# Attention over 32 sequences: the five order tables of the engines are rewritten

## The chip, the cores and the metric

The kernel runs on one core of a Trainium2 chip. The metric is the device time of one execution in microseconds, from the first to the last instruction with what lies around them; lower is better.

## What is computed

A one-layer language model tower on 32 sequences of 512 tokens, 256 channels wide. The reference, cut to what matters here:

```
h = emb_weight[x] + 2 * (lora_A[:, x].T @ lora_B.T)            # token embedding with a LoRA part
n = layernorm(h)
q, k, v = split(n @ Wqkv + bqkv)                                # 16 heads of 16 channels
local  = softmax(q k' / 4 within 64 positions) @ v
global = softmax(q k'[first 64 keys] / 4) @ v[first 64]
g = sigmoid(n @ Wg + bg)
h = h + ((1 - g) * local + g * global) @ Wout + bout
x2 = layernorm(h)
k_idx, k_probs = top_k(softmax(x2 @ router_w.T), 2)             # 8 experts, capacity limited
h = h + x2 + sum over the 2 experts of k_probs * (silu(x2 @ w1) @ w2)
```

## The kernel before, in words

The program has three stages. A short one prepares weights and tables. Then the attention stage works through the 32 sequences. Then the expert stage runs the feed-forward part over the slots of the 8 experts. Only the attention stage is touched.

In the attention stage one sequence is cut into small steps: TensorE computes tiles of scores twice, once to find the row maxima (step `max`, lines 699 to 721, 20 a sequence) and once transposed for the exponential (step `exp`, lines 741 and 748, 20 a sequence). VectorE reduces the first kind (L993, L997), ScalarE takes the exponential of the second (L903, L907), GpSimd cuts the local band out of it with two affine selects (step `sel`, L568 and L570, 16 a sequence), and TensorE multiplies with the values (step `out`, L769, L774). Around that stand the projections (`values` L795 and L800, `qk` L858, `project` L831), the transposes (`xn_t` L852 and others), the layer norms on VectorE, and the routing of the sequence two steps back.

GpSimd also issues the indirect DMAs. For each sequence there are eight gathers (step `gather`: an even argument fetches 128 rows of the LoRA table into `la`, L582, an odd one 128 rows of the embedding into `emb_t`, L585) and eight scatters (step `scatter`, L592: 128 entries of 8 bytes into the slot table). That is 16 indirect DMAs a sequence. Its other steps are `hold` (L620, an addition), `qk3` (L608), `mix` (L601), and `rstd1` and `rstd2` (L611 and L614, a power).

The order of the work is written out by hand. Each of the five engines has a table, and one pass over it issues the steps of up to seven sequences: `cur` is sequence i, `nxt` i + 1, `far` i + 2, `next` i + 3, `prev` i - 1, `past` i - 2 and `old` i - 3. The program unrolls the tables:

```
for i in range(-3, SEQ + 4):
    for flag, stage, arg in ORDER[name]:
        if 0 <= i + REL[flag] < SEQ:
            yield stage, arg, i + REL[flag]
```

So each engine's instructions stand in a fixed order, and an engine that meets a semaphore it has to wait for holds up all that is behind it on that engine. The semaphores themselves come from the data: s_ready (TensorE to VectorE, a `max` tile is complete), max_done (back), st_ready and exp_done (the same pair with ScalarE), sel_done, pv_ready and so on. In steady state one pass of a table is one sequence; below it is called a pass.

Of the kernel before, what the change touches and what calls it, by code (L numbers as in the profile page):

```python
# [89 lines left out]
def build(nc, x, emb, lora_a, lora_b, wqkv, bqkv, wout, bout, wg, bg, rw, w1, w2, y):  # L90
# [20 lines left out]
    with outer:  # L111
# [247 lines left out]
        with ExitStack() as mem:  # L359
# [8 lines left out]
            hb = tmp("hb", [P, QB, D])  # L368
# [107 lines left out]
                ("cur", "exp", 16), ("prev", "x2_t", 0), ("nxt", "max", 7), ("prev", "x2_t", 1), ("cur", "exp", 17),
                ("nxt", "m_rows", 0), ("nxt", "max", 8), ("prev", "router", None), ("cur", "out", 9), ("cur", "exp", 18),
                ("nxt", "max", 9), ("nxt", "values", 0), ("nxt", "max", 10), ("prev", "logits", None), ("cur", "exp", 19),
                ("nxt", "values", 1), ("cur", "out", 10), ("cur", "out", 11), ("nxt", "m_rows", 1), ("nxt", "values", 2),
                ("nxt", "max", 11), ("far", "xn_t", 0), ("far", "xn_t", 1), ("nxt", "exp", 0), ("nxt", "max", 12), ("far", "qk", 0),  # L480
                ("nxt", "exp", 1), ("far", "qk", 1), ("far", "qk", 2), ("nxt", "max", 13), ("far", "qk", 3), ("nxt", "exp", 2),
                ("nxt", "max", 14), ("cur", "mix", 0), ("nxt", "exp", 3), ("nxt", "out", 0), ("nxt", "max", 15), ("cur", "mix", 1),
                ("nxt", "exp", 4), ("nxt", "max", 16), ("cur", "mix", 2), ("nxt", "exp", 5), ("nxt", "max", 17), ("nxt", "out", 1),
                ("nxt", "m_rows", 2), ("nxt", "exp", 6), ("nxt", "max", 18), ("cur", "mix", 3), ("nxt", "exp", 7),
# [17 lines left out]
            ORDER["dve"] = (
                ("nxt", "max", 5), ("nxt", "cut", (0, 1)), ("prev", "scale2", 1), ("prev", "scale2", 2), ("prev", "scale2", 3),
                ("nxt", "cut", (0, 2)), ("nxt", "max", 6), ("far", "lora", 1), ("nxt", "cut", (0, 3)), ("nxt", "max", 7),
                ("far", "stats1", 0), ("nxt", "max", 8), ("far", "stats1", 1), ("prev", "shift", None), ("far", "var1", None),
                ("nxt", "max", 9), ("nxt", "kg", 1), ("nxt", "cut", (1, 0)), ("cur", "gates", None), ("nxt", "cut", (1, 1)),
                ("nxt", "gate1", None), ("nxt", "cut", (1, 2)), ("past", "rank", 5), ("far", "scale1", 0), ("prev", "logits", None),
                ("nxt", "cut", (1, 3)), ("nxt", "max", 10), ("far", "scale1", 1), ("far", "scale1", 2), ("far", "scale1", 3),
                ("nxt", "kg", 2), ("prev", "top", 0), ("nxt", "max", 11), ("nxt", "max", 12), ("far", "qk", 0), ("far", "zgate", 0),
                ("far", "qk", 1), ("prev", "top", 1), ("far", "qk", 2), ("nxt", "max", 13), ("far", "qk", 3), ("nxt", "max", 14),  # L510
                ("cur", "mix", (0, 0)), ("nxt", "cut", (2, 0)), ("cur", "mix", (0, 1)), ("nxt", "cut", (2, 1)), ("nxt", "max", 15),
                ("prev", "top", 2), ("cur", "mix", (1, 0)), ("cur", "mix", (1, 1)), ("nxt", "max", 16), ("nxt", "cut", (2, 2)),
                ("nxt", "cut", (2, 3)), ("prev", "top", 3), ("cur", "mix", (2, 0)), ("cur", "mix", (2, 1)), ("nxt", "max", 17),
                ("nxt", "max", 18), ("cur", "mix", (3, 0)), ("cur", "mix", (3, 1)), ("nxt", "max", 19), ("prev", "top", 4),
                ("nxt", "cut", (3, 0)), ("nxt", "cut", (3, 1)), ("nxt", "cut", (3, 2)), ("prev", "rank", 0), ("nxt", "cut", (3, 3)),
                ("nxt", "kg", 3), ("far", "max", 0), ("prev", "rank", 1), ("nxt", "gate2", None), ("far", "kg", 0),
                ("far", "max", 1), ("prev", "rank", 2), ("far", "zgate", 1), ("cur", "project", 0), ("far", "max", 2),
                ("next", "la_cut", 0), ("prev", "rank", 3), ("cur", "project", 1), ("next", "la_cut", 1), ("prev", "top", 5),
                ("cur", "stats2", 0), ("far", "max", 3), ("cur", "stats2", 1), ("prev", "rank", 4), ("cur", "var2", None),
# [1156 lines left out]
```

How the kernel before makes its waits and increments, by code:

```python
    def sync(self):  # L77
        self.eng.wait_ge(self.sem, self.n * self.turn + self.k)
# [5 lines left out]
def need(eng, sem, count):  # L84
    if not (isinstance(count, int) and count <= 0):
        eng.wait_ge(sem, count)
# [100 lines left out]
                @block.sync  # L188
# [5 lines left out]
                    full = VG - 1
                    whole = lora_a[:, 0:full * GT].rearrange("r (g c) -> g r c", g=full)
                    for c in range(0, GT, PIECE):
                        if c + PIECE > VOCAB - full * GT:
                            need(sp, dve_base, 1)
                        sp.dma_start(la_src[0:R * full, c:c + PIECE],
                                     whole[:, :, c:c + PIECE]).then_inc(lora_in, 16)
                    sp.dma_start(la_src[R * full:R * VG, 0:VOCAB - full * GT], lora_a[:, full * GT:VOCAB]).then_inc(lora_in, 16)
                    for c, (first, end) in enumerate(PARTS):
                        sp.wait_ge(step_copied, part_chunks[c])
                        sp.dma_start(lora_grid[:, 0:VG // 2, first:end, :], la_dst[:, 0:VG // 2, first:end, :]).then_inc(scratch_out, 16)
                    sp.wait_ge(dve_made, 3)
                    sp.dma_start(table.rearrange("(p j) w -> p j w", p=P), tab[:, :, :]).then_inc(scratch_out, 16)
                    sp.dma_start(x2_rows[N:N + P, :], zpad[:, :]).then_inc(scratch_out, 16)
                    sp.dma_start(y[N:N + P, :], zpad[:, :]).then_inc(scratch_out, 16)
                    sp.wait_ge(scratch_out, 16 * (3 + 2 * len(PARTS)))
```

## Time and profile before

| | |
|---|---|
| runs | 3893.07, 3895.12, 3898.6 us; median 3895.12 us |
| the profiled execution | 3882.32 us, span 3880.6 us |
| attention stage | about 112 us to about 2290 us of the span |
| copies of a sequence's ids on GpSimd (L577), one a pass | at 364.22 us and, 25 passes later, at 2057.27 us |
| one pass in steady state | (2057.27 - 364.22) / 25 = 67.7 us |
| mean granted TensorE clock | 0.952 |

The page divides the span in 40 slices of 97 us; the first 23 are the preparation and the attention stage, the rest is the expert stage. In the rows below a time in brackets behind a row is how long the engine sat idle before it, and what ended that wait. A row of windows gives for one stretch the busy time of each engine, then the granted TensorE clock (1.00 is 2.4 GHz, 0.50 is 1.2 GHz), the share of the DMA engines and GB/s.

### The profile page before, as it was taken

Reading aid. Unit: us, or ns where it says so; the run is one execution under the profiler, and the core shown is the slowest. Engines: PE = TensorE matmul, PEld = TensorE weight load, DVE = VectorE, ACT = ScalarE, POOL = GpSimd, SP = SyncE. Lnnn points to the kernel's source line nnn. Section 1 sums busy time; section 2 is a strip of 40 time slices with the busy share of each in tenths; the row PEclk is TensorE's granted clock in tenths of the full one; section 3 lists DMA queues with packets and bytes.
Section 4 is the critical chain, followed back from the end, with each engine's and each line's share of the span. In section 5 each row is a group of like instructions: output and inputs, shape, how many; then the busy total and the mean of one; then the engine's idle time right before and its main releaser. Section 6 shows DMA issues by size and latency. Waiting matters only on the chain. (4 is left out here: it accounts for less than half of the span.)

```text
span 3880.6 us, 117579 instructions
## 1 busy us (share of the span) xinstructions
PE 3481.5 (90%) x47537; PEld 2753.0 (71%) x47537; DVE 2172.5 (56%) x5392; ACT 1868.3 (48%) x3086; POOL 2324.1 (60%) x2599
## 2 busy tenths in 40 slices
PE   2898889888888888888899849999999999999998
PEld 1555555555555555555555539999999999999998
DVE  3576767767676776767677634343434344443333
ACT  0455555555555555555555624343444444444343
POOL 5566777777777777777776645444544444444443
PEclk7899999999999999999999969999999999999999
DMA  4354544445454444545454323232323233222222
GB/s 142 123 157 117 163 122 151 130 138 139 128 152 123 150 133 135 144 125 149 124 154 130 109 87 65 50 68 46 71 48 72 48 69 72 46 51 45 45 45 41
DMA packets 242540, 398.31 MB, mean 103 GB/s; under 512 B 34572, under 2 KB 150748, under 8 KB 242044
## 3 DMA queue, kind: packets, MB, share of 16 engines
q1 hardware_dynamic: 168540, 297.43, 25.0%
q0 software_dynamic: 70512, 91.16, 13.8%
q8 instruction: 345, 5.65, 0.6%
q10 hardware_dynamic: 3008, 2.95, 0.2%
q14 instruction: 135, 1.11, 0.1%
HBM read 198.55 MB, written 192.88 MB: 101 GB/s over the span
## 5 line engine op out<-in xcount | busy, mean ns | idle before, releaser
L1388 POOL DMA_INDIRECT out_y<-out_t,tok_out x264 | 425.7, 1612 | 747.3 <-DMA out_y<-out_t,tok_out 405.0
L1534 ACT ACTIVATE act<-psS 128x512 f32<-128x512 f32 x528 | 316.9, 600 | 882.1 <-PE psS L1462 880.9
L1596 DVE TENSOR_TENSOR h_lo<-act,h_hi 128x512 fp32r<-128x512 f32 x528 | 367.2, 695 | 562.3 <-ACT h_hi L1535 543.8
L993 DVE TENSOR_REDUCE negm<-psS 128x4 f32<-128x640 f32 x512 | 418.8, 818 | 452.3 <-remote 276.3
L903 ACT ACTIVATE pl<-psS 128x896 f32<-128x896 f32 x512 | 467.7, 913 | 379.9 <-PE psS L741 372.0
L568 POOL TENSOR_SCALAR_AFFINE_SELECT pl<-pl 128x512 f32<-128x512 f32 x512 | 354.3, 692 | 448.4 <-ACT pl L903 446.2
L1497 PE MATMUL psO<-w_hi,h_hi 128*128 128x256 f32 x2112 | 598.8, 284 | 0.8 <-DVE h_lo L1596 0.8
L1497 PE MATMUL psO<-w_lo,h_hi 128*128 128x256 f32 x2112 | 588.7, 279 | 0.0
L1497 PE MATMUL psO<-w_hi,h_lo 128*128 128x256 f32 x2112 | 587.6, 278 | 0.0
L1462 PE MATMUL psS<-xg_hi,w_hi 128*128 128x256 f32 x1984 | 551.7, 278 | 0.0
L1462 PE MATMUL psS<-xg_hi,w_lo 128*128 128x256 f32 x1984 | 551.5, 278 | 0.0
L1462 PE MATMUL psS<-xg_lo,w_hi 128*128 128x256 f32 x1984 | 551.3, 278 | 0.0
L1497 PEld LDWEIGHTS psO<-w_hi,h_hi 128*128 128x128 f32 x2112 | 397.0, 188 | 1.1 <-DVE h_lo L1596 1.0
L1497 PEld LDWEIGHTS psO<-w_lo,h_hi 128*128 128x128 f32 x2112 | 397.0, 188 | 0.0
L1497 PEld LDWEIGHTS psO<-w_hi,h_lo 128*128 128x128 f32 x2112 | 395.5, 187 | 0.0
L1462 PEld LDWEIGHTS psS<-xg_hi,w_hi 128*128 128x128 f32 x1984 | 375.1, 189 | 0.0
L1462 PEld LDWEIGHTS psS<-xg_lo,w_hi 128*128 128x128 f32 x1984 | 372.5, 188 | 0.0
L1462 PEld LDWEIGHTS psS<-xg_hi,w_lo 128*128 128x128 f32 x1984 | 372.4, 188 | 0.0
L699 PE MATMUL psS<-K,Q 96*32 96x160 bf16 (+2 forms) x8192 | 260.8, 237 | 105.7 <-DVE negm L993 71.2
L1628 DVE TENSOR_SCALAR out_t<-psO,wt_all 128x256 f32<-128x256 f32 x264 | 127.8, 484 | 360.7 <-PE psO L1497 355.8
L699 PEld LDWEIGHTS psS<-K,Q 96*32 96x32 bf16 x8192 | 165.6, 98 | 231.2 <-DVE negm L993 109.0
L570 POOL TENSOR_SCALAR_AFFINE_SELECT pl<-pl 128x512 f32<-128x512 f32 x512 | 328.0, 641 | 0.0
(232 smaller groups left out, 7728.6 us busy)
## 6 DMA issues: line engine op xcount, KB each, us to landing
qk_scr<-qk SPq DMA_DIRECT2D x64, 768.0 KB
Q<-qk_scr SPq DMA_DIRECT2D x128, 384.0 KB
K<-qk_scr SPq DMA_DIRECT2D x128, 384.0 KB
qk_scr<-qk SPq DMA_DIRECT2D x64, 512.0 KB
qk_scr<-qk SPq DMA_DIRECT2D x64, 256.0 KB
h_rows<-held SPq DMA_DIRECT2D x32, 512.0 KB
hb<-h_rows SPq DMA_DIRECT2D x32, 512.0 KB
x_rows<-x SPq DMA_DIRECT2D x32, 512.0 KB
```

The source lines that it names most:

```text
L568: pool.affine_select(out=cols[:, :, 0:P], in_=cols[:, :, 0:P], compare_op=ALU.is_ge, fill=0.0, base=0, pattern=[[0, 4], [1, P]], channel_m ...
L570: pool.affine_select(out=cols[:, :, P:WIN], in_=cols[:, :, P:WIN], compare_op=ALU.is_ge, fill=0.0, base=0, pattern=[[0, 4], [-1, P]], chan ...
L699: pe.matmul(psS[SUB * c:SUB * (c + 1), 2 + a, q % 2 * BAND + lo:q % 2 * BAND + hi], Q[0:ROWS, 4 * g + 2 * v + a, (4 * q + c) * SUB:(4 * q ...
L903: act.activation(pl[:, v, half, :, lo:hi], psS[:, 0:2, lo:hi], ACT.Exp, scale=SCALE).then_inc(exp_done, 1)
L993: dve.tensor_reduce(negm[:, g, 0, v, :, 2 * half:2 * half + 2], psS[:, 2:4, 0:2 * BAND].rearrange("p a (q u) -> p a q u", u=BAND), AX.X, A ...
L1388: pool.indirect_dma_start(out=y[:, :], in_=out_t[:, tile.out, s, :], in_offset=None, out_offset=bass.IndirectOffsetOnAxis(ap=tok_out[:, ti ...
L1462: last = pe.matmul(psS[:, f // 2, (f % 2) * 256:(f % 2) * 256 + cols], w[:, tile.par, k, fs], x[:, k, 0:cols], start=(k == 0 and n == 0), ...
L1497: last = pe.matmul(psO[:, s, 0:D], h_[:, f, ts], w[:, tile.par, f, :], start=(f == 0 and n == 0), stop=(f == FT - 1 and n == 2))
L1534: act.activation(act32[:, b, :, 0:cols], src, ACT.Silu)
L1596: dve.tensor_tensor(h_lo[:, 2 * b:2 * b + 2, 0:cols], act32[:, b, :, 0:cols], h_hi[:, 2 * b:2 * b + 2, 0:cols].bitcast(F32), ALU.subtract) ...
L1628: dve.tensor_scalar(out_t[:, tile.out, s, :], psO[:, s, 0:D], wt_all[:, bass.ds(tile.h0 + s, 1)], None, ALU.mult).then_inc(out_done, 1)
```

## The change

All five tables are replaced by new ones. They name the same steps for each sequence: no instruction of a sequence is added or taken away, no tile or semaphore changes, and the unrolling loop is the same. What changes is the order of the steps on each engine, and with it which sequences meet in a pass. In the new table of GpSimd no `gather` or `scatter` stands directly behind another. The core of the diff, of the table of GpSimd:

```diff
             ORDER["pool"] = (
...
-                ("cur", "sel", 17), ("next", "gather", 0), ("far", "rstd1", None), ("cur", "sel", 18), ("next", "gather", 1),
-                ("past", "scatter", 2), ("next", "gather", 2), ("next", "gather", 3), ("past", "scatter", 3), ("next", "gather", 4),
...
+                ("old", "scatter", 7), ("cur", "sel", 15), ("cur", "sel", 16), ("next", "gather", 0), ("cur", "sel", 17),
+                ("cur", "sel", 18), ("next", "gather", 1), ("far", "rstd1", None), ("next", "gather", 2), ("far", "hold", 0),
+                ("next", "gather", 3),
             )
```

What this makes of the program, from the steady part of the attention stage (new line numbers are 3 higher). First GpSimd, from the ids' copy that opens a sequence's gathers; L568 and L570 are the selects of one `sel`. Before:

```order
L577 COPY id_cur<-ids 128x4
L582 DMA la<-lora_rows,id_cur 128x16
L611 TENSOR_TENSOR rstd<-var,neg_half 128x4
L568 AFFINE_SELECT pl<-pl 128x4x128
L570 AFFINE_SELECT pl<-pl 128x4x128
L585 DMA emb_t<-in_L_tok_emb_weight,id_cur 128x256
L592 DMA slot_table<-entry,slot_i 41984x2
L582 DMA la<-lora_rows,id_cur 128x16
L585 DMA emb_t<-in_L_tok_emb_weight,id_cur 128x256
L592 DMA slot_table<-entry,slot_i 41984x2
L582 DMA la<-lora_rows,id_cur 128x16
L620 TENSOR_TENSOR held<-h,bout_b 128x256
```

And now, from the second gather on:

```order
L588 DMA emb_t<-in_L_tok_emb_weight,id_cur 128x256
L614 TENSOR_TENSOR rstd<-var,neg_half 128x4
L585 DMA la<-lora_rows,id_cur 128x16
L623 TENSOR_TENSOR held<-h,bout_b 128x256
L588 DMA emb_t<-in_L_tok_emb_weight,id_cur 128x256
L623 TENSOR_TENSOR held<-h,bout_b 128x256
L595 DMA slot_table<-entry,slot_i 41984x2
L571 AFFINE_SELECT pl<-pl 128x4x128
L573 AFFINE_SELECT pl<-pl 128x4x128
L595 DMA slot_table<-entry,slot_i 41984x2
```

Before, six indirect DMAs stand in a row, then one addition and a seventh. Now the same stretch has a power, an addition or two selects between any two of them.

The second place is GpSimd in the middle of a pass. Before, a gather and a scatter stood side by side there:

```order
L585 DMA emb_t<-in_L_tok_emb_weight,id_cur 128x256
L592 DMA slot_table<-entry,slot_i 41984x2
L620 TENSOR_TENSOR held<-h,bout_b 128x256
L568 AFFINE_SELECT pl<-pl 128x4x128
L570 AFFINE_SELECT pl<-pl 128x4x128
L592 DMA slot_table<-entry,slot_i 41984x2
```

And now:

```order
L588 DMA emb_t<-in_L_tok_emb_weight,id_cur 128x256
L571 AFFINE_SELECT pl<-pl 128x4x128
L573 AFFINE_SELECT pl<-pl 128x4x128
L595 DMA slot_table<-entry,slot_i 41984x2
L571 AFFINE_SELECT pl<-pl 128x4x128
L573 AFFINE_SELECT pl<-pl 128x4x128
```

The two are two selects apart. There were two more such pairs in a pass, both of two scatters; they are apart too. In the first passes, where most steps of the table fall away because their sequence does not exist, a few gathers still follow each other, and behind the last sequence 17 scatters stand in a row (16 before).

The third place is TensorE where the next sequence is normalised and projected. L800 is the last of `values`, L699 begins a `max` tile, L741 an `exp` tile; the transposes of the normalised rows (L852) and the projections (L858) follow a few rows on. Before:

```order
L774 MATMUL psO<-pg,V 32x512 x4
L807 MATMUL psX<-identb,m_cut 24x128 x4
L800 MATMUL psX<-wv_sb,xn_t 64x128 x4
L699 MATMUL psS<-K,Q 32x160 x10
L699 MATMUL psS<-K,Q 32x128
```

And now:

```order
L777 MATMUL psO<-pg,V 32x512 x4
L803 MATMUL psX<-wv_sb,xn_t 64x128 x4
L744 MATMUL psS<-Q,K 32x96
L744 MATMUL psS<-Q,K 32x128
L744 MATMUL psS<-Q,K 32x160 x2
```

The first `exp` tile of the next sequence now stands ahead of the `max` tile and the transposes; the transposes and the projections behind them keep their place among their neighbours.

## Rows read from the trace of the kernel before

**Rows 1.** The page: busy time by engine, and the granted clock in 40 slices.

```profile
PE 3481.5 (90%) x47537; PEld 2753.0 (71%) x47537; DVE 2172.5 (56%) x5392; ACT 1868.3 (48%) x3086; POOL 2324.1 (60%) x2599
...
PEclk7899999999999999999999969999999999999999
```

**Rows 2.** Windows: 25 passes of the attention stage; 200 us of the expert stage.

```profile
364.22:2057.27 1693.05, 1501.61 (x26752) 935.27 (x26752) 1179.15 (x3177) 930.52 (x1451) 1223.04 (x1576) 0.95 0.48 138
```

```profile
2400.00:2600.00 200.00, 197.22 (x1689) 196.82 (x1688) 81.11 (x160) 84.83 (x156) 92.21 (x71) 0.99 0.31 59
```

**Rows 3.** The page's groups: GpSimd's DMAs and a matmul of the expert stage.

```profile
L1388 POOL DMA_INDIRECT out_y<-out_t,tok_out x264 | 425.7, 1612 | 747.3 <-DMA out_y<-out_t,tok_out 405.0
...
L1462 PE MATMUL psS<-xg_hi,w_hi 128*128 128x256 f32 x1984 | 551.7, 278 | 0.0
```

**Rows 4.** Timeline of GpSimd in one pass: start, length, instruction, idle before.

```profile
1019.47 0.98 POOL L585 DMA_INDIRECT emb_t<-in_L_tok_emb_weight,id_cur  x1 [0.17 <-issue]
1020.76 1.01 POOL L592 DMA_INDIRECT slot_table<-entry,slot_i  x1 [0.31 <-issue]
...
1046.30 1.03 POOL L585 DMA_INDIRECT emb_t<-in_L_tok_emb_weight,id_cur  x1 [0.18 <-issue]
1047.63 1.15 POOL L592 DMA_INDIRECT slot_table<-entry,slot_i  x1 [0.30 <-issue]
...
1052.95 0.98 POOL L582 DMA_INDIRECT la<-lora_rows,id_cur  x1 [0.30 <-issue]
1053.95 0.74 POOL L620 TENSOR_TENSOR held<-h,bout_b 128x256 f32<-128x256 f32 x1
```

**Rows 5.** Timeline of TensorE in the same pass.

```profile
1019.88 0.28 PE L715 MATMUL psS<-mask,identb 128*32 128x128 bf16 x7
...
1023.15 0.46 PE L699 MATMUL psS<-K,Q 96*32 96x96 bf16 x16 [1.06 <-DVE negm L993]
...
1051.97 0.26 PE L715 MATMUL psS<-mask,identb 128*32 128x128 bf16 x3 [0.46 <-issue]
```

**Rows 6.** Timeline of VectorE in the same pass.

```profile
1022.27 0.82 DVE L993 TENSOR_REDUCE negm<-psS 128x4 f32<-128x640 f32 x1 [2.34 <-remote]
...
1055.07 0.82 DVE L993 TENSOR_REDUCE negm<-psS 128x4 f32<-128x640 f32 x1 [6.13 <-remote]
```

**Rows 7.** Windows over 27 trains of six DMAs: one of them, and the sum.

```profile
1046.35:1054.60 8.25, 6.22 (x75) 3.43 (x73) 2.59 (x12) 2.76 (x6) 6.71 (x7) 1.00 0.54 131
...
sum 219.87, PE 157.06 PEld 89.35 DVE 59.92 ACT 57.59 POOL 178.29; mean PE 5.82 PEld 3.31 DVE 2.22 ACT 2.13 POOL 6.60
```

**Rows 8.** The same over 27 pairs of DMAs: the sum.

```profile
sum 78.60, PE 64.87 PEld 45.18 DVE 41.27 ACT 6.81 POOL 64.33; mean PE 2.40 PEld 1.67 DVE 1.53 ACT 0.25 POOL 2.38
```

**Rows 9.** The same over 27 DMAs that stand alone: the sum.

```profile
sum 43.20, PE 38.52 PEld 24.83 DVE 29.10 ACT 21.07 POOL 38.33; mean PE 1.43 PEld 0.92 DVE 1.08 ACT 0.78 POOL 1.42
```

**Rows 10.** The same over 25 DMAs behind one addition: one, and the sum.

```profile
376.67:378.27 1.60, 1.25 (x13) 0.48 (x14) 0.00 (x0) 0.00 (x0) 0.93 (x1) 0.50 0.00 1
sum 40.00, PE 28.60 PEld 14.93 DVE 0.92 ACT 7.10 POOL 23.20; mean PE 1.14 PEld 0.60 DVE 0.04 ACT 0.28 POOL 0.93
```

**Rows 11.** Waits over the 25 passes: us in total, times, longest.

```profile
PE psS L699 <- DVE negm L993: 56.8, 69, 1.1
PE psX L817 <- DVE mix L1096: 13.0, 25, 0.5
```

```profile
DVE negm L993 <- remote: 242.4, 49, 8.0
```

**Rows 12.** Timeline of TensorE where the queries and keys are projected.

```profile
1124.21 3.60 PE L858 MATMUL psX<-xn_t,wqk 128*128 128x512 f32 x4
1127.74 0.46 PE L741 MATMUL psS<-Q,K 102*32 102x96 bf16 x16
1128.13 3.70 PE L858 MATMUL psX<-xn_t,wqk 128*128 128x512 f32 x8
```

**Rows 13.** Windows: a stretch at the lower clock.

```profile
1056.00:1059.40 3.40, 3.40 (x30) 1.79 (x30) 0.83 (x1) 1.51 (x3) 2.21 (x3) 0.53 0.14 41
```

**Rows 14.** GpSimd's selects over the 25 passes: busy, mean ns, idle before.

```profile
L568 POOL TENSOR_SCALAR_AFFINE_SELECT pl<-pl 128x512 f32<-128x512 f32 x400 | 277.3, 693 | 337.7 <-ACT pl L903 335.6 <-issue 1.5
```

More of the change, by code:

```diff
@@ L476, in build @@
[L476 to L484, printed above, removed]
@@ new lines, in build @@
+                ("nxt", "exp", 0), ("nxt", "max", 11), ("far", "xn_t", 0), ("far", "xn_t", 1), ("nxt", "exp", 1),
+                ("nxt", "max", 12), ("far", "qk", 0), ("far", "qk", 1), ("nxt", "max", 13), ("far", "qk", 2), ("far", "qk", 3),
+                ("nxt", "exp", 2), ("nxt", "max", 14), ("cur", "mix", 0), ("nxt", "out", 0), ("nxt", "max", 15), ("nxt", "exp", 3),
+                ("cur", "mix", 1), ("nxt", "exp", 4), ("nxt", "max", 16), ("cur", "mix", 2), ("nxt", "exp", 5), ("nxt", "out", 1),
@@ L487, in build @@
+                ("nxt", "max", 17), ("nxt", "m_rows", 2), ("nxt", "exp", 6), ("cur", "mix", 3), ("nxt", "exp", 7),
+                ("nxt", "max", 18), ("nxt", "out", 2), ("nxt", "exp", 8), ("nxt", "max", 19), ("cur", "attn_t", 0),
+                ("cur", "attn_t", 1), ("nxt", "exp", 9), ("prev", "ahead", None), ("far", "max", 0), ("nxt", "out", 3),
+                ("nxt", "m_rows", 3), ("far", "max", 1),
             )
             ORDER["act"] = (
-                ("cur", "exp", 11), ("cur", "evac", (1, 0)), ("cur", "exp", 12), ("far", "embed", None), ("cur", "exp", 13),
@@ L504, in build @@
[L504 to L519, printed above, removed]
-                ("prev", "top", 6), ("far", "max", 4), ("next", "lora", 0), ("far", "cut", (0, 0)), ("cur", "scale2", 0),
+                ("prev", "mix", (2, 0)), ("prev", "mix", (2, 1)), ("past", "top", 4), ("cur", "max", 17), ("cur", "gates", None),
@@ L539, in build @@
+                ("cur", "qk_write", (0, 2)), ("cur", "qk_write", (1, 0)), ("cur", "qk_write", (1, 1)), ("cur", "qk_write", (1, 2)),
+                ("cur", "load", 0), ("prev", "m_out", 2), ("prev", "m_in", 2), ("old", "y", None), ("prev", "m_out", 3),
+                ("cur", "load", 1), ("prev", "m_in", 3), ("cur", "hold", None), ("cur", "load", 2), ("cur", "m_out", 0),
+                ("cur", "m_in", 0), ("cur", "load", 3), ("past", "x2", None), ("cur", "m_out", 1),
             )
```

76 lines of the change are left out of this document (46 added, 30 removed).

## The prediction

> **What bounds the kernel now.** I began with the page. TensorE is busy 90% of the span and no other engine above 60% [rows 1], so the question is where TensorE loses the rest. The windows answer it by stage: in the expert stage it is busy 197.22 of 200 us at full clock, in 25 passes of the attention stage 1501.61 of 1693.05 us at a mean clock of 0.95 [rows 2]. So a pass of 67.7 us holds 191.44 / 25 = 7.66 us of idle TensorE, and a clock of 0.95 between the levels 1.00 and 0.50 is 10% of the pass, 6.8 us, at the lower one. The expert stage has GpSimd's indirect DMAs too, of 1.6 us each, and TensorE shows no idle time before its matmuls of 278 ns [rows 3]. It is not in the change, and I leave it at nothing.
>
> Next I looked at who ends TensorE's idle time. Two things repeat in every pass. One is the wait for VectorE's row maxima, 56.8 us in 25 passes, 2.27 us a pass [rows 11]. The other is called "issue": TensorE waits for nothing that the profile shows. I laid the timelines of three engines side by side. In GpSimd's train of six DMAs, which starts at 1046.30 and issues one every 1.3 us [rows 4], TensorE's tiny matmuls of L715 come in clumps with gaps of 0.46 us [rows 5]. Their results are late as well: the `max` tile whose last matmuls run at 1051.97 to 1052.23 is reduced by VectorE only at 1055.07, after 6.13 us of idleness ended by "remote" [rows 6], which is 2.1 us after the start of the train's last DMA at 1052.95. The same happens at the pair of DMAs at 1019.47 and 1020.76: the tile is complete at 1020.16, VectorE starts at 1022.27, 1.5 us behind the second DMA's start, and TensorE then waits 1.06 us for the maxima [rows 4 to 6]. VectorE's waits on "remote" are 49 in 25 passes, 242.4 us [rows 11], two a pass, one for this pair and one for the train. I read it so: while GpSimd's indirect DMAs are being issued, TensorE's semaphores go out late and its small instructions are slowed; a DMA that starts before the one ahead is through prolongs it.
>
> What that costs was measured by windows from a DMA's start to 1.60 us past the last one's start. TensorE is idle (219.87 - 157.06) / 27 = 2.33 us in a train of six [rows 7], (78.60 - 64.87) / 27 = 0.51 us in a pair [rows 8], (43.20 - 38.52) / 27 = 0.17 us at a DMA alone [rows 9], and (40.00 - 28.60) / 25 = 0.46 us at the DMA that follows the train behind one addition, 1.9 us after the one before [rows 10].
>
> **The change, term by term, for one pass.** A pass has 16 indirect DMAs: the train, the one behind it, three pairs and three alone.
>
> A, TensorE's idle time at the DMAs. Now: 2.33 + 0.46 + 3 x 0.51 + 3 x 0.17 = 4.83 us. In the new table none is adjacent. Five stand behind only one power, addition or mix, about 1.9 to 2.2 us after the one before (1.0 us of DMA, 0.15 to 0.2 us of issue and 0.74 us or 1.05 us of work); eleven are further apart. The eleven cost 0.17 us each, 1.87 us. The nearest row for the five is 0.46 us [rows 10], but that one comes out of a train, so it is their upper bound; the lower is 0.17 us. The total is 2.72 to 4.17 us; I take the middle, 3.45. Gain 1.4 us, bounds 0.7 and 2.1.
>
> The Trainium skill (DMA: Bandwidth & Descriptors, section Latency and other measured facts) has as its best guess for slow DMA engines a contention at the ports in front of the descriptor rings, which all engines fetch from. That load goes with the number of descriptors, which the change leaves alone; by it A would be nothing. No row here shows a port.
>
> B, late maxima. The wait of 1.06 us behind the pair goes, since the pair let go of the result 1.5 us behind its second start, and a DMA alone should do so 1.5 us behind its only one, mostly while VectorE has other work. Bounds: nothing, and all 2.27 us of such waits. I take 1.05 us.
>
> C, the clock. It falls once a pass, directly behind the train: the stretch from 1056.00 is at 0.53 with TensorE busy all the time [rows 13]. What it costs is seen at the projections: four records of L858 take 3.60 us at the lower clock, eight take 3.70 us at the full one [rows 12], so 1.75 us lost in 3.6 us. The other 3.2 us hold small tiles, for which no row gives a price. Bounds: nothing, if the clock still falls, and 3.4 us, half of 6.8. I take 2.0 us, because the 8 us ahead of the fall, in which TensorE sits idle 2.33 us and more, are what the change breaks up.
>
> D, the new order's own waits. No row of before shows them. GpSimd's selects now stand behind single DMAs more often, 1.2 us each, but they wait for ScalarE 335.6 / 25 = 13.4 us a pass [rows 14], and that hides it; without this cover each of them would pass its 1.2 us on to an `out` step and so to TensorE. The stages on TensorE are the same, and what idles outside A and B today is 7.66 - 4.83 - 1.05 = 1.8 us. A wait of the size of that for VectorE's mix, 13.0 / 25 = 0.5 us [rows 11], may come once more: I take a loss of 0.5 us, bounds 0 and 1.8.
>
> SP's table is shifted as well. Its DMAs are the same ones, the DMA engines are 48% busy [rows 2], and no wait of TensorE on a load stands in the rows, so nothing is booked.
>
> Sum: 1.4 + 1.05 + 2.0 - 0.5 = 3.95 us a pass. The trains of six stand in 27 passes; in the first passes and behind the last sequence DMAs are still adjacent and I book nothing. 27 x 3.95 = 107 us. The profiled execution took 3882.3 us and would take 3775; the median of the runs is 3895.1, 13 us above it, so the same difference gives 3788 us.
>
> **The rivals.**
>
> The clock still falls. The transposes L852 and the projections keep their place, and the train's place is taken by four DMAs some 2 us apart. Then C is nothing: 1.95 x 27 = 53 us, 3842 us. For it speaks that the clock fell in all passes, whatever else varied; against it, that at the pair, with its wait of 1.06 us, it did not fall.
>
> The price belongs to each DMA wherever it stands: spreading the train spreads the stall. Then A and C are nothing and B less D leaves 0.55 x 27 = 15 us, 3880 us. The DMAs alone at 0.17 us against 2.33 / 6 = 0.39 us in the train speak against it. The Trainium skill's rule above, in DMA: Bandwidth & Descriptors, would make it so.
>
> More than booked: A, B and C at their upper bounds and D at nothing, 2.1 + 2.27 + 3.4 = 7.8 us a pass, 210 us, 3685 us.
>
> Slower than before: separate stalls are dearer than one long one. In a train TensorE's held results come out together, and it is stopped once; each of 16 separate DMAs may catch a tile in flight. If each costs what the one behind the addition costs, 0.46 us, A becomes 4.83 - 7.36, a loss of 2.5 us; if the clock falls as before and B gives nothing, that is 27 x 2.5 = 68 us, 3963 us. The point that decides is a mean price of 4.83 / 16 = 0.30 us; the loose ones measured 0.17.
>
> **How the numbers follow.** Forecast of 3788, between 3735 and 3835: 0.50. Clock still falls, 3842 within 3835 to 3865: 0.19. Price per DMA, 3865 to 3900: 0.10. More than booked, below 3735: 0.09. Slower, above 3900: 0.12. I predict 3788 us. The range from 3710 to 3885 leaves out the slower case and parts of its two neighbours and of the lowest. A difference under 0.2%, 8 us, can't be told from none: faster by more than that 0.84, within it 0.05, slower 0.11.
>
> **What would show it.** A: windows of 1.60 us at each DMA, with 3 to 4 us of idle TensorE in a pass in place of 4.83. B: VectorE's waits on "remote" shrink to about 1.5 us at the longest, and the 6.13 us one is gone; TensorE's wait for the maxima falls from 2.27 to about 1.2 us a pass. C: granted clock near 1.00 in the passes, and every L858 four at 1.85 us. D: TensorE's list of waits has no new name above 0.5 us a pass. The copies of the ids should come every 63.8 us. I would be wrong if the pass is shorter but the clock row is unchanged (C), if the windows at the close DMAs show 0.46 us or more (A), or if selects appear late, with `out` waiting for them (D).

## The result and the profile after

| | before | after |
|---|---|---|
| runs | 3884.02 to 3898.6 us, median 3894.1 | 3672.51 to 3681.65 us, median 3679.2 |
| ratio | 1 | 0.9449, 95% interval 0.9427 to 0.9471 |
| span of the profiled execution | 3880.6 us | 3677.1 us |
| one pass | 67.7 us | (1856.2 - 346.0) / 25 = 60.4 us |

The change made the kernel 5.5% faster, 215 us; 3788 us were forecast, with a range down to 3710. The page after, busy time by engine and the granted clock in 40 slices; its counterpart is [rows 1]:

```profile
PE 3365.1 (92%) x47537; PEld 2719.6 (74%) x47537; DVE 2215.0 (60%) x5392; ACT 1853.3 (50%) x3086; POOL 2312.7 (63%) x2599
...
PEclk7799999999999999999999699999999999999999
```

Windows over 25 passes and over 200 us of the expert stage, the counterpart of [rows 2]:

```profile
346.00:1856.20 1510.20, 1400.61 (x26751) 904.49 (x26748) 1214.96 (x3176) 917.92 (x1451) 1214.06 (x1576) 1.00 0.52 154
2400.00:2600.00 200.00, 198.39 (x1717) 198.14 (x1715) 82.49 (x162) 87.58 (x160) 94.78 (x74) 1.00 0.31 59
```

A pass lost 7.3 us: 4.0 us of busy TensorE (60.06 to 56.02), though its matmuls are the same, and 3.3 us of idle TensorE (7.66 to 4.38). The granted clock went from 0.95 to 1.00: in windows of 2 us over the 25 passes, the lower clock takes 7.2 us of a pass before and 0.1 us after. The expert stage is as it was. Next GpSimd's timeline where the ids' copy opens a sequence's gathers, the counterpart of [rows 4]: starts are 1.9 us apart and more, here 2.9 and 2.0 us.

```profile
1015.52 0.96 POOL L588 DMA_INDIRECT emb_t<-in_L_tok_emb_weight,id_cur  x1 [0.15 <-issue]
1017.09 1.10 POOL L614 TENSOR_TENSOR rstd<-var,neg_half 128x4 f32<-128x4 f32 x1 [0.62 <-DVE var L1205]
1018.39 1.00 POOL L585 DMA_INDIRECT la<-lora_rows,id_cur  x1 [0.20 <-issue]
1019.42 0.78 POOL L623 TENSOR_TENSOR held<-h,bout_b 128x256 f32<-128x256 f32 x1
1020.36 0.98 POOL L588 DMA_INDIRECT emb_t<-in_L_tok_emb_weight,id_cur  x1 [0.16 <-issue]
```

Windows of 1.60 us from the start of each DMA that begins 1.7 to 2.3 us behind the one before it, 96 in these 25 passes: one of them, and the sum (compare [rows 9] and [rows 10]):

```profile
357.39:359.00 1.61, 1.40 (x47) 1.13 (x38) 0.07 (x1) 0.80 (x3) 0.98 (x1) 1.00 0.77 274
...
sum 153.60, PE 149.16 PEld 101.85 DVE 72.18 ACT 73.54 POOL 120.65; mean PE 1.55 PEld 1.06 DVE 0.75 ACT 0.77 POOL 1.26
```

TensorE idles (153.60 - 149.16) / 96 = 0.05 us at such a DMA, at a spacing at which 0.46 us had been read before the change, behind a train. Over all 400 DMAs of these passes it is 0.05 us as well. TensorE's largest waits in the same 25 passes:

```profile
PE psX L810 <- DVE m_cut L1019: 18.8, 25, 1.0
PE psS L744 <- ACT pl L906: 17.7, 39, 1.1
PE psS L751 <- ACT pl L906: 12.7, 43, 0.6
...
PE psS L702 <- DVE negm L996: 8.2, 25, 0.3
```

VectorE has no wait on "remote" left (242.4 us in [rows 11]), and its longest wait for a `max` tile is 2.4 us where it was 8.0.

### The profile page after: what moved, and what is told of

It is laid out like the page before. It is cut to its first block and busy times, and to the rows that moved or that the text cites. A ratio compares the mean times of both kernels' runs of the same rounds, so it can differ in the third digit from the quotient of the medians.

```text
span 3677.1 us, 117607 instructions
## 1 busy us (share of the span) xinstructions
PE 3365.1 (92%) x47537; PEld 2719.6 (74%) x47537; DVE 2215.0 (60%) x5392; ACT 1853.3 (50%) x3086; POOL 2312.7 (63%) x2599
## 5 line engine op out<-in xcount | busy, mean ns | idle before, releaser
L571 POOL TENSOR_SCALAR_AFFINE_SELECT pl<-pl 128x512 f32<-128x512 f32 x512 | 342.7, 669 | 233.2 <-ACT pl L906 232.4
L573 POOL TENSOR_SCALAR_AFFINE_SELECT pl<-pl 128x512 f32<-128x512 f32 x512 | 330.1, 645 | 0.0
L1538 ACT ACTIVATE h_hi<-psS 128x512 fp32r<-128x512 f32 x528 | 312.9, 593 | 0.0
L1356 POOL DMA_INDIRECT xg<-x_rows,tok_in x245 | 253.6, 1035 | 74.8 <-issue 74.8
```

Source lines behind the costliest of these rows:

```text
L571: pool.affine_select(out=cols[:, :, 0:P], in_=cols[:, :, 0:P], compare_op=ALU.is_ge, fill=0.0, base=0, pattern=[[0, 4], [1, P]], channel_m ...
L573: pool.affine_select(out=cols[:, :, P:WIN], in_=cols[:, :, P:WIN], compare_op=ALU.is_ge, fill=0.0, base=0, pattern=[[0, 4], [-1, P]], chan ...
L1356: pool.indirect_dma_start(out=rows[:, s, :], out_offset=None, in_=x2_rows[:, :], in_offset=bass.IndirectOffsetOnAxis(ap=tokens[:, s:s + 1] ...
L1538: act.activation(h_hi[:, 2 * b:2 * b + 2, 0:cols], src, ACT.Silu).then_inc(silu_done, 1)
```

## The experiments

Nearly every expectation weighs the same theories: the time between the starts of GpSimd's indirect DMAs is what was changed (theory 1 nearly throughout), against the number of DMAs, the order of the other engines, or DMAs merely standing elsewhere.

**One table alone, DMAs apart.** The kernel before with a GpSimd table of mine in which no DMA is adjacent to another; the four other tables stay. Its core:

```diff
-                ("cur", "sel", 13), ("past", "scatter", 0), ("past", "scatter", 1), ("cur", "sel", 15), ("cur", "sel", 16),
+                ("cur", "sel", 11), ("cur", "sel", 12), ("past", "scatter", 0), ("prev", "rstd2", None),
+                ("past", "scatter", 1), ("cur", "sel", 13), ("past", "scatter", 2), ("cur", "sel", 15),
```

> The kernel before with a new table for GpSimd alone, in which no indirect DMA follows another; the four other tables are those of before. Theory 1 (the adjacency of GpSimd's indirect DMAs costs the time, through held results, slowed matmuls and the clock that falls behind them; the other tables matter little): a pass of 60.3 to 62 us instead of 67.7, granted clock near 1.00 in the passes, ratio to the kernel before 0.945 to 0.96. Theory 2 (the rewritten order of the other four engines brings most of it): a pass of 66 to 68 us, ratio 0.98 to 1.00.

Measured: 3866.9 us, ratio 0.9936 (0.9919 to 0.9953), a pass of 67.0 us. Time and pass lie where theory 2 had them. The waits of GpSimd and TensorE between 300 and 1950 us (lines are 1 higher than before):

```profile
PE psS L700 <- DVE negm L994: 70.2, 51, 2.0
PE psO L770 <- POOL pl L571: 69.8, 38, 3.2
...
POOL slot_table L593 <- DVE entry L1078: 29.9, 24, 2.9
```

The trains are gone, and with them VectorE's waits on "remote". But a scatter that now stands ahead of the power waits for VectorE, the selects behind it come late, and `out` waits for them, 3.2 us at the longest. TensorE idles 8.0 us of a pass, more than before, and the lower clock takes 9.6 us of it. Late selects with `out` waiting for them are what the prediction feared in D. Spreading DMAs in one table isn't enough; steps they push back must have slack on the engines that wait for them. No run has one of the new tables beside old ones, so what each of them adds is not shown.

**An instruction between, too short to matter, and one that is long.** The kernel before, nothing moved, with one instruction between adjacent DMAs: first a memset of one column, which fits in the gap, so that starts stay 1.3 us apart; then an addition of 128x256, starts 1.9 us apart.

```diff
+                    dma, spaced = False, 0
                     for stage, arg, s in order("pool"):
+                        if dma and (stage == "scatter" or stage == "gather" and arg > 0):
+                            need(pool, pad_done, spaced)
+                            spaced += 1
+                            pool.tensor_tensor(pad[:, :], bout_b[:, :], wg_b[:, :], ALU.add).then_inc(pad_done, 1)
+                        dma = stage in ("scatter", "gather")
```

> The kernel before, all tables as they were, with a memset of one column on GpSimd between every two adjacent indirect DMAs; nothing is moved. Theory 1a (what counts is the time between the starts of two DMAs: the next must not start before the one ahead has let go, some 1.4 us behind its start): the starts are 1.5 to 1.6 us apart instead of 1.3, so the stall shrinks by a half or more, ratio 0.96 to 0.99. Theory 1b (what counts is that another instruction stands between, whatever its length): ratio 0.945 to 0.96. Theory 2 (order of the other engines): ratio 1.00.

Measured: 3897.5 us, ratio 1.0016 (1.0004 to 1.0029). A neighbour of another kind does nothing. The starts did not come 1.5 us apart as expected, so the run says nothing on spacing.

> The kernel before, all tables as they were, with an addition of 128x256 elements (0.74 us) on GpSimd between every two adjacent indirect DMAs; nothing is moved, eight such additions are added to a pass, 6 us of GpSimd's time. Theories 1a and 1b: the starts are 1.9 us apart and the stalls are gone, clock near 1.00, ratio 0.95 to 0.97 (some of the 6 us may show). Theory 2: ratio 1.00 to 1.02.

Measured: 3786.1 us, ratio 0.9737 (0.9716 to 0.9758): half of the gain, with eight additions more a pass and no step moved, and a ratio that neither theory had. No wait on "remote" is left, so the late results are gone. What probably kept the rest is seen on VectorE, groups between 300 and 1950 us:

```profile
L567 POOL TENSOR_TENSOR pad<-bout_b,wg_b 128x256 f32<-128x256 f32 x207 | 154.1, 745 | 4.4
L1019 DVE TENSOR_TENSOR m_rest<-negm,m_cut 128x32 f32<-128x32 f32 x103 | 137.5, 1335 | 1.2
```

and in its waits:

```profile
PE psS L706 <- DVE negm L1000: 117.9, 62, 3.8
```

The subtraction of 128x32 takes 1335 ns; in the kernel after the same form takes 232 ns. VectorE is busy 53.1 us of a pass, 47.2 before; of the 5.9 us between them this subtraction has 4.3. TensorE waits for the maxima, and the lower clock still takes 5.3 us of a pass. That the one causes the other is argued from these numbers.

**Shorter spacers.** The same with an addition of 128x96, then with a select of 128x256, both of about 0.4 us; starts come 1.6 us apart.

```diff
+                            pool.tensor_tensor(pad[:, 0:96], bout_b[:, 0:96], wg_b[:, 0:96], ALU.add).then_inc(pad_done, 1)
...
+                            pool.affine_select(out=pad[:, :], in_=wg_b[:, :], compare_op=ALU.is_ge, fill=0.0, base=0,
+                                               pattern=[[1, 256]], channel_multiplier=0).then_inc(pad_done, 1)
```

> The kernel before with an addition of 128 rows of 96 columns between any two of GpSimd's DMAs that were neighbours, where the earlier run had 256 columns, so that starts are about 1.6 us apart and not 1.9. It adds work that the computation doesn't need. Theory 1 (a hold lasts about 1.5 us from the start of a DMA, and anything beyond that is free): the train costs as little as with 1.9 us, and since the additions are shorter the time is at or below the 3786 us of the longer ones, 3740 to 3790. Theory 2 (the price falls slowly with distance): about half way, 3820 to 3860, with 1.0 to 2.0 us of idle time per train. Theory 3 (the number of DMAs matters, not the distance): 3890.

> The kernel before with a select of 128 rows of 256 columns, in place of the addition, between any two neighbouring DMAs of GpSimd; it adds work that the computation doesn't need. A select reads one operand where the addition reads two. Theory 1 (what kept the run with additions 107 us above the changed kernel is that VectorE's own operations go slower beside GpSimd's additions, 240 ns to 1363 ns for one of them): with selects VectorE's busy time per pass stays near 47 us and the time comes to 3700 to 3740 us. Theory 2 (what is missing is that the GpSimd's later steps come late, by the time that eight further operations take): about 3786 again, the waits for the GpSimd's selects grown and VectorE's time no matter.

Measured: 3744.5 us, ratio 0.9642 (0.9626 to 0.9659), and 3723.2 us, 0.9584 (0.9562 to 0.9607); a later run of the select beside another series of the kernel before gave 3752.4 us, 0.9655 (0.9604 to 0.9706), above the 3710 to 3730 that was expected.

> The kernel before with the select of 128 rows of 256 columns between neighbouring DMAs (3723 us, ratio 0.9584 in its series), once more; the selects are work that the computation doesn't need. Theory 1: where the kernel before takes about 3670 us the spacing has little left to free and the selects cost what they cost: 3640 to 3700, ratio 0.99 to 1.01; where it takes 3890, again 3710 to 3730. Theory 2: ratio 0.958 in either case.

Groups of the run with short additions, then of the first run with selects:

```profile
L567 POOL TENSOR_TENSOR pad<-bout_b,wg_b 128x96 f32<-128x96 f32 x211 | 85.3, 404 | 4.8
L1019 DVE TENSOR_TENSOR m_rest<-negm,m_cut 128x32 f32<-128x32 f32 x105 | 32.5, 309 | 1.0
```

```profile
L567 POOL TENSOR_SCALAR_AFFINE_SELECT pad<-wg_b 128x256 f32<-128x256 f32 x212 | 88.7, 418 | 2.4
L1019 DVE TENSOR_TENSOR m_rest<-negm,m_cut 128x32 f32<-128x32 f32 x106 | 49.5, 467 | 1.0
```

Both take the subtraction down to 309 and 467 ns. The form of the spacer (two operands or one) made no difference that these two show; the length, 745 against 404 and 418 ns, is what they share. My theory on additions is not borne out. Between 63% and 76% of the gain came with nothing moved. But at 1.6 us the stall isn't gone. Here are VectorE's waits in the two runs:

```profile
DVE negm L1000 <- remote: 55.8, 17, 3.8
```

```profile
DVE negm L1000 <- remote: 73.9, 23, 3.8
```

and windows over 24 and 23 of the six DMAs that were a train:

```profile
sum 229.27, PE 196.99 PEld 115.05 DVE 83.40 ACT 120.14 POOL 207.10; mean PE 8.21 PEld 4.79 DVE 3.47 ACT 5.01 POOL 8.63
```

```profile
sum 221.52, PE 204.97 PEld 115.55 DVE 86.23 ACT 122.53 POOL 197.97; mean PE 8.91 PEld 5.02 DVE 3.75 ACT 5.33 POOL 8.61
```

TensorE idles 1.35 and 0.72 us in six DMAs whose starts are 1.6 us apart, where it was 2.33 us at 1.3 us. The idle time of 1.35 us is what theory 2 of the run with short additions named, though the time was theory 1's. At 1.9 us (long additions) no "remote" is left. So the price falls between 1.3 and 1.9 us and doesn't end at 1.6.

**Adjacency put back into the new order.** The kernel after with GpSimd's steps moved: (a) six DMAs in one train; (b) three pairs; (c) both, which is the adjacency of before. The other four tables are the new ones.

```diff
# (a)
-                ("nxt", "hold", 1), ("old", "scatter", 0), ("cur", "sel", 0), ("old", "scatter", 1), ("cur", "sel", 1),
+                ("old", "scatter", 0), ("old", "scatter", 1), ("far", "gather", 4), ("nxt", "hold", 1), ("cur", "sel", 0),
...
+                ("cur", "sel", 18), ("far", "rstd1", None), ("far", "hold", 0), ("next", "gather", 1),
+                ("next", "gather", 2), ("next", "gather", 3),
# (b)
...
+                ("prev", "mix", 3), ("far", "gather", 7), ("old", "scatter", 3), ("cur", "sel", 6), ("cur", "sel", 7),
+                ("cur", "sel", 8), ("old", "scatter", 4), ("old", "scatter", 5), ("nxt", "hold", 3), ("cur", "sel", 10),
+                ("cur", "sel", 11), ("old", "scatter", 6), ("old", "scatter", 7), ("cur", "sel", 12), ("cur", "sel", 13),
```

> The changed kernel with six of its 16 indirect DMAs of a pass pulled together into one train at the place where the train stood before; the other ten stay apart, the four other tables are the changed ones. Theory 1: TensorE's results are held for some 8 us again, VectorE idles 5 to 6 us, the clock falls behind it: 3 to 6 us a pass above the changed kernel, ratio to the kernel before 0.965 to 0.99. Theory 2: within 1% of the changed kernel, ratio 0.945 to 0.955.

> The changed kernel with three pairs of its 16 DMAs pulled together in each pass (gather 7 with scatter 3, scatters 4 and 5, scatters 6 and 7), no train; the four other tables are as changed. Theory 1 (each DMA that starts 1.3 us behind another has a price of its own, so a pair costs what the three pairs did before the change, 0.5 us each in TensorE's idle time, and some clock): the pass goes from 60.4 to about 62 us, the whole to 3720 to 3740, a ratio to the kernel before of 0.955 to 0.960. Theory 2 (the holds of TensorE add up along a train, and a pair alone hardly holds it): 3680 to 3695, ratio 0.945 to 0.949, low clock under 0.5 us per pass. Theory 3 (the new order as a whole is what counts, any DMA moved costs): over 3740.

> The changed kernel with a train of six DMAs and three pairs in each pass, which is the adjacency of the kernel before on the new order of the five tables. Theory 1 (how DMAs stand to each other is all that the change is worth): it comes back to the kernel before, pass 67.5 to 68.3 us, 3870 to 3895 us, ratio 0.994 to 1.001, clock low for 6 to 7 us per pass. Theory 2 (the order of the other four engines carries part of the gain by itself): it stays where the train alone left it, 3838 to 3850, ratio 0.986 to 0.989, or between the two, and the distance to 3893 is what the other tables are worth.

> The run with the train of six and three pairs on the new order (3895 us, ratio 1.0035 in its series), once more. Theory 1: within 1% of the kernel before of this series, whatever that takes, since both have the same close starts; on a chip where these cost little, what is left between the two is the order alone. Theory 2: 3895 us in any case.

| close starts a pass | us | ratio, interval | one pass | TensorE busy | idle | at the lower clock |
|---|---|---|---|---|---|---|
| none (after) | 3679.2 | 0.9449 (0.9427 to 0.9471) | 60.4 us | 56.0 | 4.4 | 0.1 |
| 3, in pairs (b) | 3731.3 | 0.9621 (0.9603 to 0.9638) | 62.4 us | 56.0 | 6.4 | 1.0 |
| 5, in a train (a) | 3838.2 | 0.9866 (0.9849 to 0.9883) | 66.1 us | 58.7 | 7.4 | 5.7 |
| 8 (c) | 3895.0 | 1.0035 (1.0020 to 1.0051) | 68.4 us | 59.3 | 9.1 | 7.5 |
| 8 (c), again | 3901.9 | 1.0024 (1.0011 to 1.0038) | 68.4 us | 59.3 | 9.2 | 7.4 |

The last three columns are us of a pass, over 25 passes. The rows come from different series. With the adjacency of before the new order takes the time of before. So the new order gains nothing as long as the close starts are there. A close start costs 2.0 / 3 = 0.67 us of a pass in a pair and 5.7 / 5 = 1.1 us in a train (0.8 and 1.2 us if worked out from the ratios). In idle time of TensorE the two are alike, 2.0 / 3 = 0.67 and 3.0 / 5 = 0.60 us; what makes the train dearer is 2.7 us more of busy TensorE, with 5.7 us at the lower clock. Three pairs leave the clock nearly alone. TensorE's timeline in one train of (c), where GpSimd starts DMAs at 981.60, 982.94, 984.20, 985.45, 986.78 and 988.08:

```profile
985.80 0.21 PE L712 MATMUL psS<-mask,identb 128*32 128x32 bf16 x2 [0.37 <-issue]
985.84 0.24 PE L718 MATMUL psS<-mask,identb 128*32 128x128 bf16 x2
987.23 0.27 PE L718 MATMUL psS<-mask,identb 128*32 128x128 bf16 x5 [1.15 <-issue]
988.65 0.22 PE L718 MATMUL psS<-mask,identb 128*32 128x128 bf16 x1 [1.15 <-issue]
```

VectorE in the same place:

```profile
990.36 0.82 DVE L996 TENSOR_REDUCE negm<-psS 128x4 f32<-128x640 f32 x1 [7.31 <-PE psS L718]
```

TensorE waits for nothing that the profile names, 1.15 us twice, and VectorE gets the finished tile at 990.36, 1.5 us after the end of the matmul at 988.65 and 2.3 us after the train's last start. That is the picture of [rows 5] and [rows 6], made at will.

**The two kernels once more, unchanged, in one series.** This gives two traces with the same window of 300 to 1950 us, in which the lost time can be laid out by instruction.

> The kernel before, unchanged, for a trace of its own beside the runs below. In the last series the kernel before took 3670.9 us where in three others it took 3881.6 to 3894.1, and the distance between its DMAs' starts is set by the program. Theory 1 (the price of a start 1.3 us behind another differs from chip to chip, and the kernel before is faster only where that price is small): where it takes about 3670 us, its trains idle TensorE for well under the 2.3 us of [rows 7] and the clock is low for well under 7 us per pass; where it takes about 3890 us, both are as they were. Theory 2 (something else on that chip is faster, such as memory or the expert stage): the idle time at trains and the low clock are as in [rows 7], and the gain lies outside the attention stage.

> The changed kernel, unchanged, beside the kernel before in the same series. Theory 1: where the kernel before takes about 3670 us, close starts cost little there, and the change gains 1 to 3%, 3600 to 3640 us; where it takes about 3890 us, the change comes out at 3660 to 3685 as before, ratio 0.943 to 0.947. Theory 2 (the chip is faster in something else): the ratio is 0.945 in either case, 3470 us where the kernel before takes 3670.

Measured: 3897.1 us, ratio 1.0009 (0.9996 to 1.0023), pass 68.1 us; and 3678.8 us, 0.9448 (0.9428 to 0.9467), pass 60.4 us. Groups of TensorE in the kernel before, 24.2 passes (line and form, busy us, mean ns, idle before):

```profile
L858 PE MATMUL psX<-xn_t,wqk 128*128 128x512 f32 x387 | 225.4, 722 | 0.0
L715 PE MATMUL psS<-mask,identb 128*32 128x128 bf16 x3088 | 147.8, 225 | 41.7 <-issue 40.5 <-ACT m_t L931 1.2
...
L699 PE MATMUL psS<-K,Q 96*32 96x96 bf16 x772 | 103.2, 212 | 35.3 <-DVE negm L993 28.9 <-issue 3.2 <-DMA K<-qk_scr 1.0
L741 PE MATMUL psS<-Q,K 102*32 102x96 bf16 x770 | 99.8, 212 | 0.1
L748 PE MATMUL psS<-Q,KG 102*64 102x512 bf16 x384 | 59.7, 391 | 0.0
L852 PE MATMUL psX<-ident,xn 128*128 128x128 f32 x200 | 49.7, 357 | 48.4 <-issue 39.1 <-ACT V L924 6.8 <-ACT m_t L931 2.3
L807 PE MATMUL psX<-identb,m_cut 128*24 128x128 bf16 x388 | 38.0, 220 | 0.0
```

The same in the kernel after, 27.3 passes:

```profile
L861 PE MATMUL psX<-xn_t,wqk 128*128 128x512 f32 x448 | 207.2, 605 | 2.7
L718 PE MATMUL psS<-mask,identb 128*32 128x128 bf16 x3496 | 144.3, 219 | 1.3 <-issue 1.1
...
L744 PE MATMUL psS<-Q,K 102*32 102x96 bf16 x872 | 110.0, 207 | 21.3 <-ACT pl L906 20.3 <-issue 0.2
L702 PE MATMUL psS<-K,Q 96*32 96x96 bf16 x872 | 109.8, 207 | 2.4 <-issue 0.3
L751 PE MATMUL psS<-Q,KG 102*64 102x512 bf16 x436 | 67.8, 386 | 13.3 <-ACT pl L906 13.2
L810 PE MATMUL psX<-identb,m_cut 128*24 128x128 bf16 x436 | 43.5, 222 | 29.8 <-DVE m_cut L1019 19.9 <-DVE mix L1099 9.9
L855 PE MATMUL psX<-ident,xn 128*128 128x128 f32 x216 | 33.8, 283 | 3.4 <-issue 2.1
```

Busy and idle together, divided by the passes: the mask matmuls 7.8 to 5.3 us, the transposes of xn 4.1 to 1.4, the projections 9.3 to 7.7, the first score tiles 5.7 to 4.1: 8.4 us gained. The transposed scores 4.1 to 4.8, L748 2.5 to 3.0, the m_cut transposes 1.6 to 2.7: 2.3 us lost to new waits. That is 6.1 of the 7.7 us between these two traces; the rest is spread over many rows.

**Three DMAs more, of 128 or 16 rows.** The kernel after with three further gathers a pass, each right behind another DMA, into a tile that nobody reads.

```diff
+                        if s >= 0 and (stage, arg) in (("gather", 7), ("scatter", 4), ("scatter", 6)):
+                            need(pool, pad_in, 16 * extra)
+                            extra += 1
+                            pool.indirect_dma_start(out=pad[0:128, :], out_offset=None, in_=emb[:, :],
+                                                    in_offset=bass.IndirectOffsetOnAxis(ap=ids[0:128, 0:1], axis=0)).then_inc(pad_in, 16)
```

> The changed kernel with three DMAs more per pass, each a gather of 128 rows into a tile that nobody reads, right behind gather 7, scatter 4 and scatter 6: work that the computation doesn't need. It is the measure for the run with 16 rows. Theory 1 (a start 1.3 us behind another costs, whatever it moves): like the three pairs, 3731 us, or more by what 4 us of further GpSimd work a pass bring in late selects, 3730 to 3790. Theory 2 (rows cost): the same here, since the rows are there.

> The changed kernel with the same three further DMAs per pass, of 16 rows instead of 128: work that the computation doesn't need. Theory 1 (a price of the start): the same time as with 128 rows, within 10 us. Theory 2 (a price of each row's descriptors, an eighth of them here): an eighth of what the three full ones add to 3679 us, so 3685 to 3695.

> The changed kernel with three further gathers of 128 rows per pass right behind others (3649 us in a series where the kernel before took 3671), once more; they are work that the computation doesn't need. Theory 1 (a close start costs what a pair did, 0.65 us each, and the chip of that series had a smaller price): where the kernel before takes about 3890 us, 3730 to 3800; where it takes 3671, again about 3650. Theory 2 (the price was small there because these DMAs are not waited for by anything): 3680 to 3700 on either.

> The same three further gathers with 16 rows instead of 128 (3623 us in the same earlier series); they are work that the computation doesn't need. Theory 1 (the price is of the start, not of the rows): within 15 us of the run with 128 rows, so 3720 to 3800 where the kernel before takes 3890. Theory 2 (the price goes by rows): 3685 to 3700 there, an eighth of what the full ones add.

Measured: 128 rows 3648.8 us, ratio 0.9939 (0.9913 to 0.9964), again 3648.2 us, 0.9930 (0.9905 to 0.9956); 16 rows 3623.3 us, 0.9884 (0.9852 to 0.9916), again 3624.2 us, 0.9861 (0.9827 to 0.9894). All of them were below the 3679 us of the kernel without these DMAs, because both series ran on a chip on which the kernel before took 3670.9 and 3675.1 us, where it took 3881.6 to 3897.1 in all other series. In the second of them, windows over 82 and 83 pairs of DMAs, 128 rows and then 16; and last those of (b), 80 pairs on one of the other chips:

```profile
sum 237.28, PE 222.10 PEld 154.19 DVE 209.66 ACT 170.70 POOL 211.06; mean PE 2.71 PEld 1.88 DVE 2.56 ACT 2.08 POOL 2.57
```

```profile
sum 239.95, PE 222.30 PEld 146.37 DVE 209.55 ACT 174.79 POOL 210.85; mean PE 2.68 PEld 1.76 DVE 2.52 ACT 2.11 POOL 2.54
```

```profile
sum 231.54, PE 183.17 PEld 122.91 DVE 106.14 ACT 94.03 POOL 206.64; mean PE 2.29 PEld 1.54 DVE 1.33 ACT 1.18 POOL 2.58
```

TensorE idles 0.19, 0.21 and 0.60 us in a pair. So a pair costs a third as much on that chip, for reasons that no run shows; the second DMA of a pair is the added one there and a real one in (b), so the comparison isn't clean. On that chip the idle time doesn't depend on the rows: an eighth of the rows idles TensorE as long. The rows have a price of their own, 25 and 24 us for 96 DMAs, where theory 1 had allowed 10 and 15 us. Whether rows count where close starts are dear is open, and so is what the change gains on that chip, since it did not run there.

**Two more on that chip.** (c) with the select of 128x256 between neighbouring DMAs, and the kernel before with a select of 128x64, starts 1.4 to 1.5 us apart.

> The run with the train of six and three pairs on the new order (3895 us), and between any two neighbouring DMAs a select of 128 rows of 256 columns, so that starts are 1.6 us apart; the selects are work that the computation doesn't need. Theory 1 (the whole loss of that run is the 1.3 us between starts): 3690 to 3740 us, ratio 0.948 to 0.961, clock low for under 1.5 us per pass, no idle time in the trains. Theory 2 (part of the loss is that DMAs and the steps around them stand early or late in the table): above 3780, with waits for GpSimd's or VectorE's results in its place.

> The kernel before with a select of 128 rows of 64 columns between neighbouring DMAs, so that starts come between 1.3 and 1.6 us apart; the selects are work that the computation doesn't need. Theory 1 (the price ends where starts are further apart than a hold lasts, about 1.45 us): a time at or near the 3723 us of 256 columns if the distance comes out at 1.45 us or above, and near 3880 if below. Theory 2 (an instruction that really occupies the engine between two DMAs is enough at any length): 3700 to 3730 whatever the distance.

Measured: 3738.1 us, ratio 1.0191 (1.0152 to 1.0230), and 3634.0 us, 0.9890 (0.9850 to 0.9930). The first number lies in theory 1's range only by the accident of the chip; by the ratio it missed. TensorE waits for VectorE:

```profile
PE psX L817 <- DVE m_cut L1026: 42.9, 50, 1.4
PE psS L731 <- DVE negm L1003: 37.7, 25, 1.7
```

The selects put in at these places may cost what they save; (c) without them did not run on that chip, so this isn't shown. In the second the trains of six leave no idle time at all (229.40 us busy of 229.40 in 26 windows), at a spacing closer than the 1.6 us that still idled TensorE elsewhere. It beats the kernel before by 1.1%; whether 1.45 us is enough where close starts are dear was not tried.

## Why the prediction was wrong

What was right: the place and the mechanism (results of TensorE held while indirect DMAs start closely), the direction, the clock that falls behind the train, and that no stage but attention moves. The sizes were wrong, and the three gains all the same way: 3.95 us a pass were booked, 7.3 us came, 27 x 7.3 = 197 us of the 204 by which the two spans differ.

**A, the step that failed most.** "I take the middle, 3.45" for what the DMAs would still cost. Measured after: 0.05 us for each of the 16, 0.75 us in all, below the lower bound of 2.72. Neither price in that step held. The 0.46 us of [rows 10] come out of a train and carry its backlog (the one shown there is at clock 0.50). The 0.17 us of [rows 9] were to be DMAs that stand alone, but seven of the 27 windows are the DMA behind the addition (376.67 of [rows 10] is one of them); they hold 2.98 of the 4.68 us, and the other twenty idle 1.70 / 20 = 0.09 us. Over all 75 DMAs alone in the 25 passes it is 0.12 us. With that, the DMAs cost 2.33 + 0.46 + 3 x 0.51 + 3 x 0.12 = 4.68 us before, and A is 4.68 - 0.75 = 3.93 us, nearly twice its upper bound. Why a DMA alone costs 0.05 us now, and not the 0.12 us of before, stays open. That a spaced start is nearly free is what the run with long additions shows too, 1.9 us apart: TensorE idled 0.06 us at a DMA, by windows over 208 of them.

**B.** 1.05 us booked; the wait for the maxima went from 2.27 to 8.2 / 25 = 0.33 us, so 1.94 us, near the upper bound of 2.27. Some of it may be counted in A as well: at the pair of [rows 5], 0.27 us of the 1.06 us lie inside the window.

**C.** 2.0 us booked, at most 3.4. Busy TensorE fell by 4.04 us. The clock no longer falls in the passes; with 7.1 us less at the lower clock, and the lower clock at half speed, it accounts for at most 3.6 us of this. Of the fall, 9.29 to 7.40 us are the projections. The small tiles, for which "no row gives a price", had one: the mask matmuls went from 6.08 to 5.29 us a pass, 48 to 41 ns each of pipelined busy time. Part of them stands inside the trains, at clock 1.00 [rows 7], so this isn't the clock alone; the two were not separated.

**D.** 0.5 us of loss booked, bounds 0 and 1.8. Idle time fell by 3.28 us where A and B make 5.87, so D is 2.59 us by difference, above its bound; (18.8 + 17.7 + 12.7) / 25 = 2.0 us of it are waits for m_cut and for the exponentials. The waits for the exponentials are the new order's own: in (c), where the stalls are back, they are as large, (31.4 + 1.4) / 24.1 = 1.4 us a pass against 1.2. Those for m_cut are 9.6 / 24.1 = 0.4 us there against 0.75, so the stall hides a part of them at most. The largest of these waits in (c):

```profile
PE psS L751 <- ACT pl L906: 31.4, 46, 1.4
```

Sum: 3.93 + 1.94 + 4.04 - 2.59 = 7.3. D was under-booked too, and this error went the other way: with D booked right the forecast would have been further off.

**The rivals.** "More than booked" (3685 us, 0.09) is nearest in time, but by luck: it had D at nothing and A at 2.1 us, and A and C beyond their bounds made up for D. "The clock still falls" and "separate stalls are dearer" fell with the clock row and the windows. "The price belongs to each DMA" fell with (c) against the kernel after: the same DMAs and descriptors in both, and 3901.9 against 3678.8 us in one series. The best guess of the Trainium skill cited there (DMA: Bandwidth & Descriptors, section Latency and other measured facts) is on slow DMA engines. Read as the prediction read it, as a load that goes with the number of descriptors, it would give no difference between the two, and the measurement decides against that reading for this stall.

## What to carry to other kernels

Where TensorE idles at "issue" in small matmuls and VectorE's or ScalarE's waits end in "remote", look at GpSimd for indirect DMAs that start 1.3 us apart. Spacing of 1.6 us took 63 to 76% of the gain here, and 1.9 us by work that is there anyway took the stall away. A spacer of 0.4 us on GpSimd tells in one run whether a new order can gain. Check that steps pushed back by it have slack. And price a stall from rows that lie outside the disturbance one wants to remove, and check each window of such a sum: what is read next to a train belongs to the train.

## What the runs showed of the hardware that was not expected

A close start costs 0.67 us of a pass in pairs and 1.1 us in a train of six. TensorE's idle time at it is about the same in both (0.67 and 0.60 us); the train adds 5.7 us at the lower clock, three pairs 1.0 us. At 1.6 us between starts a part of the stall is left (0.7 to 1.4 us in six DMAs), at 1.9 us and more 0.05 us at a DMA. On one chip of those used the stall was smaller (0.19 against 0.60 us in a pair, none in six DMAs 1.45 us apart), and the kernel before took 3671 and 3675 us there, and 3882 to 3897 elsewhere. A subtraction of 128x32 on VectorE took 232 ns in the kernel after and 1335 ns beside additions of 745 ns on GpSimd; what the two engines share was not looked into.
